# Context attentions as one block: normalisation, operands and, in the first, the combination of routed rows

## The reference, cut to what matters

```python
x = x + _L1_ffn_ref(_layernorm(x), ...)     # each row to one expert of 8, times its probability
x = x + _L2_xattn_ref(_layernorm(x), ctx, ctx, mask, ...)
...
x = x + _L3_xattn_ref(_layernorm(x), ctx, ctx, mask, attn_bias, ...)
x = x + _L3_ffn_ref(_layernorm(x), ...)

# both context attentions: q from x, k and v from the context (77 rows for each of B = 2 sequences)
q = split_heads(queries @ Wq + bq); k = split_heads(keys @ Wk + bk); v = split_heads(values @ Wv + bv)
scores = q @ k.T / sqrt(HD)      # 16 heads of HD = 16
ctx = softmax(masked scores) @ v;  return ctx @ Wo + bo
```

## Time and profile before

| | us |
|---|---|
| executions, median of 3 | 3460.03 |
| lowest, highest | 3453.24, 3462.03 |
| the profiled execution, its own time | 3466.94 |
| its span, first to last instruction | 3465.3 |

### The profile page before, as it was taken

One profiled execution on the slowest core, in us unless ns is written; L12 is line 12 of the kernel. 1 busy time (PEld: TensorE's weight loads), 2 busy tenths in 40 slices (PEclk: granted clock), 3 DMA queues, 4 the chain that ended last, 5 costly groups with the idle time before them and its releaser, 6 DMA issues. The chain is left out here.

```text
span 3465.3 us, 68349 instructions
## 1 busy us (share of the span) xinstructions
PE 2923.5 (84%) x26674; PEld 2032.6 (59%) x26675; DVE 2086.9 (60%) x3094; ACT 1894.2 (55%) x2864; POOL 1298.7 (37%) x941
## 2 busy tenths in 40 slices
PE   6679997735779998979998595979999999988596
PEld 3246665314436666536666595666666666657595
DVE  6968887485768774867783223756444444466222
ACT  3458885282448885548884111656555555456131
POOL 2259996020127885237873212630000000045212
PEclk9979998867889999989998798979999999989698
DMA  4511111100012220022222511011000000042612
GB/s 160 209 54 54 54 56 59 73 0 19 13 43 55 53 53 22 1 48 59 53 50 77 176 36 51 2 31 49 25 25 25 26 25 1 1 102 50 234 36 68
DMA packets 218052, 193.21 MB, mean 56 GB/s; under 512 B 126837, under 2 KB 176865, under 8 KB 216737
## 3 DMA queue, kind: packets, MB, share of 16 engines
q1 hardware_dynamic: 210247, 172.30, 17.2%
q0 software_dynamic: 5280, 14.42, 1.3%
q10 hardware_dynamic: 2233, 2.39, 0.2%
HBM read 112.72 MB, written 39.00 MB: 44 GB/s over the span
## 5 line engine op out<-in xcount | busy, mean ns | idle before, releaser
L2578 POOL TENSOR_TENSOR lta_p_lo<-lta_p,lta_p_hi 128x1024 f16<-128x1024 f32 x256 | 538.9, 2132 | 221.6 <-DVE lta_p_hi L2701 221.6
L2773 ACT ACTIVATE lta_p<-lta_banks,lt_gmax 128x512 f32<-128x512 f32 x512 | 323.7, 682 | 113.0 <-PE lta_banks L2616 108.5
L2684 DVE TENSOR_REDUCE lta_s_ps<-lta_s_ps 128x1 f32<-128x1101 f32 x240 | 314.2, 1309 | 106.8 <-PE lta_s_ps L2595 106.8
L3717 PE MATMUL m_h_ps<-m_x,m_w 128*128 128x512 f16 x1536 | 356.5, 383 | 4.1 <-issue 4.1
L3729 PE MATMUL m_y_ps<-m_w,m_hT 128*128 128x256 f16 x3072 | 355.8, 273 | 2.3 <-DVE m_hT L3887 2.3
L3887 DVE TENSOR_TENSOR m_hT<-m_h,m_hT 128x512 f16<-128x512 f32 x256 | 177.0, 692 | 281.1 <-ACT m_hT L3814 279.4
L3814 ACT ACTIVATE m_h<-m_h_ps,m_h_bias,m_h_scale 128x512 f32<-128x512 f32 x256 | 199.3, 778 | 266.0 <-PE m_h_ps L3717 257.8
L3729 PEld LDWEIGHTS m_y_ps<-m_w,m_hT 128*128 128x128 f16 x3072 | 298.9, 98 | 65.9 <-issue 8.6
L1227 POOL TENSOR_TENSOR c0a_tri_p_lo<-c0a_tri_p,c0a_tri_p_hi 128x1024 f16<-128x1024 f32 (+2 forms) x192 | 285.5, 1524 | 58.5 <-DVE c0a_tri_p_hi L1401 57.8
L3717 PEld LDWEIGHTS m_h_ps<-m_x,m_w 128*128 128x128 f16 x1536 | 151.1, 99 | 163.0 <-issue 10.6
L1476 ACT ACTIVATE c0a_tri_p<-c0a_banks,c_size 128x512 f32<-128x512 f32 (+3 forms) x384 | 208.3, 576 | 45.6 <-PE c0a_banks L1295 34.3
(11 more groups left out here) (758 smaller groups left out, 6574.7 us busy)
## 6 DMA issues: line engine op xcount, KB each, us to landing
m_w<-in_L_ffn_w_dram SPq DMA_DIRECT2D x4, 8192.0 KB, 39.0
m_raw<-in_L_ffn_W_dram SPq DMA_DIRECT2D x16, 1024.0 KB, 6.5
lta_q<-ltb_qT SPq DMA_DIRECT2D x96, 128.0 KB, 2.4
c_side<-in_fside_Bx16xSxS_dram SPq DMA_DIRECT2D x16, 616.0 KB, 4.9
c0a_tri_q<-c_near SPq DMA_DIRECT2D x96, 96.0 KB
c0a_tri_k<-c_mixed SPq DMA_DIRECT2D x93, 96.0 KB
lta_k<-ltb_kT SPq DMA_DIRECT2D x64, 137.6 KB, 2.5
lt_vh<-ltb_v SPq DMA_DIRECT2D x64, 128.0 KB
```

Source lines behind the costliest of these rows:

```text
L2578: nc.gpsimd.tensor_tensor(p_lo[:, slot, :], p32[:, p32_slot(h, j), :], p_hi[:, slot, :], ALU.subtract).then_inc(rested, 1)
L2684: nc.vector.tensor_reduce(ntop_of(h)[:, n:n + 1], scores(h, n), AX_X, ALU.max, negate=True).then_inc(top_ready, 1)
L2773: nc.scalar.activation(p32[0:rows, slot, c * 512:(c + 1) * 512], t_ps[0:rows, c, :], ACT.Exp, bias=bias, scale=p["gmax"][0:rows, 0:1]).the ...
L3717: last = nc.tensor.matmul(h_ps[:, f % RING, :], w1[:, v, a, c, f * P:(f + 1) * P], x16[:, b, c, n * CHUNK:(n + 1) * CHUNK], start=c == 0 a ...
```

## The change

The separate normalisation block of the context attentions goes; `cross_operands` becomes one block that normalises, turns and projects in four groups of four tiles (`CHUNK = 4`). In the first attention (`combine` is given) the combination of the routed rows is part of the same block as well: GpSimd issues the gathers there, VectorE combines and sums four tiles, makes their statistics, and ScalarE normalises the tiles of groups 0 to 2 (by a shift and a scale), VectorE those of group 3. The context's keys and values come first on TensorE, and each group's queries directly behind its turned tiles (`lag` 0). In the second attention the statistics stay one chain and VectorE normalises all tiles; keys and values come behind the first group of turned tiles, and a group's queries behind the next group's (`lag` 1). In both, the last group's queries stand behind the maximum of the values, which is now taken over partitions by a transpose, a VectorE maximum over 128 numbers, and a product that spreads it (the all-reduce on GpSimd goes). Queries have a ring of two banks, turned tiles one of three. Every load has its own semaphore. The products that make `kbd` move from VectorE to GpSimd; two memsets move the other way. `slot` and `weight` live outside the feed-forward's stage, so that stage is left ahead of the combination; for the last feed-forward `combine_experts` is called behind it and computes as before.

```diff
-def routed_ffn_stage(nc, env, tag, args, name, func, biased, capacity, out=None):
+def routed_ffn_stage(nc, env, tag, args, name, func, biased, capacity, slot, weight):
...
-        slot = st.sb("slot", [P, TILES], U32)
-        weight = st.sb("weight", [P, TILES])
...
-        with ExitStack() as inner:
-            combine_experts(nc, env, Stage(nc, inner, tag + "c"), inner, sorted_y, slot, weight, out)
+    return sorted_y
...
-def combine_experts(nc, env, st, ctx, sorted_y, slot, weight, out):
...
+def combine_experts(nc, env, tag, sorted_y, slot, weight, out):
+    with ExitStack() as ctx:
+        st = Stage(nc, ctx, tag)
+        yg = st.sb("yg", [P, TILES, D])
+        gathered = env.gathered.pop()
+        added, stored = st.sem("added"), st.sem("stored")
+        block = ctx.enter_context(nc.Block())
...
-            if out is None:
-                dve.wait_ge(added, t + 1)
-                nc.vector.bn_stats(env.stats[:, t, :], env.x[:, t, :]).then_inc(summed, 1)
-        dve.wait_ge(added, TILES)
-        if out is None:
-            dve.wait_ge(summed, TILES)
...
-def cross_attention_stage(nc, env, tag, args, name, mask, side, hides):
+def cross_attention_stage(nc, env, tag, args, name, mask, side, hides, combine=None):
...
+    CHUNK, TURNED, NORMED = 4, 3, 4
+    groups = T // 512
+    lag = 1 if combine is None else 0
...
-    layernorm_stage(nc, env, st.tag + "l", env.x, dst_T=xT)
+    rows = sb("rows", [P, NORMED, D])
...
-        sp.dma_start(wk[:], mat("Wk")).then_inc(kv_loaded, 16)
-        sp.dma_start(wv[:], mat("Wv")).then_inc(kv_loaded, 16)
-        sp.dma_start(bk[:], col("bk"), allow_slow_non_contiguous=True).then_inc(kv_loaded, 16)
-        sp.dma_start(bv[:], w("bv").partition_broadcast(P)).then_inc(kv_loaded, 16)
-        sp.dma_start(wq[:], mat("Wq")).then_inc(q_loaded, 16)
-        sp.dma_start(bq[:], col("bq"), allow_slow_non_contiguous=True).then_inc(q_loaded, 16)
+        sp.dma_start(wk[:], mat("Wk")).then_inc(wk_loaded, 16)
+        sp.dma_start(wv[:], mat("Wv")).then_inc(wv_loaded, 16)
+        sp.dma_start(wq[:], mat("Wq")).then_inc(wq_loaded, 16)
+        sp.dma_start(bq[:], col("bq"), allow_slow_non_contiguous=True).then_inc(bq_loaded, 16)
+        sp.dma_start(bk[:], col("bk"), allow_slow_non_contiguous=True).then_inc(bk_loaded, 16)
+        sp.dma_start(bv[:], w("bv").partition_broadcast(P)).then_inc(bv_loaded, 16)
...
-        nc.gpsimd.memset(v_top[:], 0.0).then_inc(v_set, 1)
-        nc.gpsimd.memset(v16[:, :, :, HD:HD + 1], 1.0).then_inc(v_set, 1)
...
+        if combine is not None:
+            for t in range(TILES):
+                nc.gpsimd.indirect_dma_start(yg[:, t, :], None, sorted_y, bass.IndirectOffsetOnAxis(ap=slot[:, t:t + 1], axis=0)
+                                             ).then_inc(gathered[t], 16)
...
-        pool.wait_ge(v_topped, 1)
-        nc.gpsimd.partition_all_reduce(v_max[:], v_top[:], P, RMAX).then_inc(v_reduced, 1)
+        pool.wait_ge(ind_made, 1)
+        for c in range(DC):
+            pool.wait_ge(k_ready, c + 1)
+            for b in range(B):
+                nc.gpsimd.tensor_tensor(kbd[:, c, b, :].rearrange("p (h j) -> p h j", h=half),
+                                        spread(kT[:, c:c + 1, b * NCTX:(b + 1) * NCTX], [P, half, NCTX]),
+                                        spread(ind[:, :].unsqueeze(2), [P, half, NCTX]), ALU.mult).then_inc(kbd_ready, 1)
+        pool.wait_ge(kbd_ready, DC * B)
...
+        def turn(t):
+            pe.wait_ge(normed, t + 1)
+            if t >= TURNED:
+                pe.wait_ge(x_evac, t - TURNED + 1)
+            for c in range(DC):
+                last = nc.tensor.transpose(x_ps[:, t % TURNED, c * P:(c + 1) * P], rows[:, t % NORMED, c * P:(c + 1) * P],
+                                           env.ident[:])
+            last.then_inc(x_turned, 1)
+
+        def queries(n):
+            if n == 0:
+                pe.wait_ge(wq_loaded, 16)
+            pe.wait_ge(x_evac, CHUNK * (n + 1))
+            for f in range(DC):
+                i = DC * n + f
+                if i >= 2:
+                    pe.wait_ge(q_evac, i - 1)
+                for c in range(DC):
+                    last = nc.tensor.matmul(q_ps[:, i % 2, :], wq[:, c, f * P:(f + 1) * P], xT[:, c, n * 512:(n + 1) * 512],
+                                            start=c == 0, stop=c == DC - 1)
+                last.then_inc(q_done, 1)
+
+        def context():
+            pe.wait_ge(wk_loaded, 16)
+            pe.wait_ge(ctx_evac, 1)
+            for f in range(DC):
+                for c in range(DC):
+                    last = nc.tensor.matmul(k_ps[:, f * B * NCTX:(f + 1) * B * NCTX], wk[:, c, f * P:(f + 1) * P],
+                                            ctxT[:, c, :], start=c == 0, stop=c == DC - 1)
+            last.then_inc(k_done, 1)
+            pe.wait_ge(wv_loaded, 16)
...
+        if lag == 0:
+            context()
+        for g in range(groups):
+            for t in tiles_of(g):
+                turn(t)
+            if g == 0 and lag == 1:
+                context()
+            if g >= lag and g < groups - 1:
+                queries(g - lag)
+        if lag == 1:
+            queries(groups - 2)
+        pe.wait_ge(v_topped, 1)
+        nc.tensor.transpose(c_ps[0:1, 0:P], v_top[:], env.ident[:]).then_inc(top_turned, 1)
+        pe.wait_ge(peaked, 1)
+        nc.tensor.matmul(c_ps[:, P:P + 1], env.ones[0:1, :], peak[0:1, 0:1], start=True, stop=True).then_inc(peak_spread, 1)
+        queries(groups - 1)
...
+        def spread_std(g, part):
+            act.wait_ge(var_ready, g + 1)
+            nc.scalar.activation(rstd[:, part], var[:, part], ACT.Sqrt).then_inc(std_ready, 1)
+
+        def normalise(t):
+            if t >= NORMED:
+                act.wait_ge(x_turned, t - NORMED + 1)
+            nc.scalar.activation(rows[:, t % NORMED, :], env.x[:, t, :], ACT.Identity, bias=shift[:, t:t + 1],
+                                 scale=rstd[:, t:t + 1]).then_inc(normed, 1)
+
+        def keep_rows(t):
+            act.wait_ge(x_turned, t + 1)
...
+        if combine is None:
+            spread_std(0, slice(0, TILES))
+        for g in range(groups):
+            if combine is not None:
+                spread_std(g, slice(g * CHUNK, (g + 1) * CHUNK))
+                if g < groups - 1:
+                    act.wait_ge(rstd_ready, 2 * (g + 1))
+                    for t in tiles_of(g):
+                        normalise(t)
+            for t in tiles_of(g):
+                keep_rows(t)
+            if g:
+                keep_queries(g - 1)
+        keep_queries(groups - 1)
...
+        def group_stats(g, part):
+            merge_stats(nc, step, mean[:, part], var[:, part], env.stats[:, part, :], D)
+            nc.vector.tensor_scalar(var[:, part], var[:, part], LN_EPS, None, ALU.add).then_inc(var_ready, 1)
+            dve.wait_ge(std_ready, g + 1)
+            nc.vector.reciprocal(rstd[:, part], rstd[:, part]).then_inc(rstd_ready, 1)
+            dve.wait_ge(rstd_ready, SHIFTED * g + 1)
+
+        def complete(t):
+            dve.wait_ge(gathered[t], 16)
+            nc.vector.scalar_tensor_tensor(env.x[:, t, :], yg[:, t, :], weight[:, t:t + 1], env.x[:, t, :], ALU.mult,
+                                           ALU.add).then_inc(added, 1)
+            if t % CHUNK:
+                sum_row(t - 1)
+
+        def sum_row(t):
+            dve.wait_ge(added, t + 1)
+            nc.vector.bn_stats(env.stats[:, t, :], env.x[:, t, :]).then_inc(summed, 1)
+
+        def scale_bias():
+            dve.wait_ge(bq_loaded, 16)
+            nc.vector.tensor_scalar(bqs[:], bq[:], HD ** -0.5, None, ALU.mult).then_inc(bqs_ready, 1)
+
+        def normalise(t):
+            if t >= NORMED:
+                dve.wait_ge(x_turned, t - NORMED + 1)
+            nc.vector.tensor_scalar(rows[:, t % NORMED, :], env.x[:, t, :], mean[:, t:t + 1], rstd[:, t:t + 1],
+                                    ALU.subtract, ALU.mult).then_inc(normed, 1)
...
+        def halve_values():
+            link = chain(dve, v_linked)
+            dve.wait_ge(top_turned, 1)
+            nc.vector.tensor_reduce(peak[:], c_ps[0:1, 0:P], AX_X, ALU.max).then_inc(peaked, 1)
+            dve.wait_ge(peak_spread, 1)
+            link(nc.vector.tensor_scalar(v_max[:], c_ps[:, P:P + 1], TINY, None, ALU.max))
...
+        nc.vector.memset(v_top[:], 0.0).then_inc(v_set, 1)
+        nc.vector.memset(v16[:, :, :, HD:HD + 1], 1.0).then_inc(v_set, 1)
+        if combine is None:
+            SHIFTED = 1
+            group_stats(0, slice(0, TILES))
+            for t in range(TILES):
+                normalise(t)
+                if t == 8:
+                    scale_bias()
+                if t == 12:
+                    keep_values()
+            keep_keys()
+            halve_values()
+            hide()
         else:
...
+            SHIFTED = 2
+            for g in range(groups):
+                part = slice(g * CHUNK, (g + 1) * CHUNK)
```

(24 more changed lines are left out.)

158 lines of the change are left out of this document (74 added, 84 removed).

## The result

| | us |
|---|---|
| before, median of 4 (lowest, highest) | 3460.23 (3453.24, 3462.03) |
| changed, median of 4 (lowest, highest) | 3435.89 (3432.49, 3441.12) |
| ratio, 95% interval | 0.9935, 0.9914 to 0.9955 |
| the changed kernel's profiled execution, its span | 3441.12, 3439.5 |

24.3 us faster by the medians; 26 were forecast, and the time lies in the forecast's range. The profiled execution is the slowest of the four.

A forecast was written before the change was run, and what follows sets the result against it. Bounds: GpSimd's gathers in the combination, then barriers and load waits, TensorE at the operands' end. Gains of 18.7 (Part A) and 7.7 (Part B), 26.4, taken as 26, off median 3460 gave 3434 us; range 3425 to 3446.

The forecast's parts named there:

- Part A: Routed rows' combination, normalisation and operands of the first context attention: 59.6 us, to gain 18.7, bounds 14 to 20.5.
- Step 1: Before the first gather: clear moved ahead of the combination, +0.4, and GpSimd's constant, +0.5 us.
- Step 2: First four tiles: fourth gather issued 3.8 later, combined 2.8 after issue; loads delaying first gathers 0.5 (0 to 2).
- Steps 2 to 4: VectorE's groups: 0.99 a tile, statistics chain 2.03, shift 0.21, so 6.2 a group; VectorE takes over from gathers' 5.03.
- ScalarE is free when a root is asked for: First attention: ScalarE normalises 12 tiles, about 0.4 each, and no root has to wait for it.
- Steps 5 to 7: First attention's tail: last tiles normalised 1.46, keys, values, maximum's hop 0.9, last queries 3.47, copy, clear; GpSimd products hidden.
- The clock: First attention: 1.0 us taken off for query group 3 of 4 meeting a slow TensorE clock (0 to 3.5).
- R1: Rival: every first-attention query group runs at 1.2 GHz, 6.9 us a group; time 3438.5; chance 0.10.
- R3: Rival: gathers starve, their issues held by VectorE's two-input SBUF reads; gain gone at 3.4 a gather; chance 0.05.
- Part B: Normalisation and operands of the last context attention, TensorE the bound: 37.5 us, to gain 7.7, bounds 5 to 9.5.
- R2: Rival: last attention wins nothing, turns between query groups each stalling TensorE two us; time 3441; chance 0.06.
- R4: Rival: no overlap, no group normalised or projected until all sixteen tiles are combined; time 3452; chance 0.02.

The follow-up runs named there:

- again: The changed kernel run once more, unedited, beside the follow-up kernels: 3436.65 us, ratio 0.9925 to the kernel before.
- plain_rows: Changed kernel with the 16 indirect gathers replaced by plain transfers on SP, rows' permutation left out (measurement only): 3434.06 us, ratio 0.9913.
- a_end: Changed kernel with query groups 0 to 2 of the first context attention placed behind all turned tiles and row copies: 3445.32 us, ratio 0.9957.
- loads_late: Changed kernel with SP's loads from wq on held until the fourth gather has landed, first attention: 3438.3 us, ratio 0.9931.
- preload: Changed kernel with the first attention's seven loads issued in the routed feed-forward behind the expert weights, into own buffers: 3460.5 us, ratio 0.9991.

## Why the prediction was right, point by point

The time came out 2 us from the forecast, but in A errors of opposite sign met, and the closeness is in part luck: the medians differ by 0.6 to 3.5 more than the two stretches account for. Times after the first gather:

| | predicted | changed | again |
|---|---|---|---|
| chain of group 0 starts | 8.0 | 10.8 | 11.2 |
| group 1 | 14.4 | 15.9 | 16.2 |
| group 2 | 20.6 | 24.9 | 23.6 |
| group 3 | 26.8 | 29.8 | 28.8 |
| last tiles' normalisation starts | 28.9 | 34.4 | 31.7 |
| last queries start | 33.4 | 39.7 | 36.9 |
| table load | 38.5 | 45.0 | 42.3 |

**Part A.**
- Step 1 (+0.9 before the first gather): from store to gather 6.28 in place of 5.54, +0.7. Right.
- Step 2 (first group 8.0 after the first gather): my 8.0 has a slip of 0.4, since its terms give 3.8+2.8+1.0 = 7.6. Measured are 7.8 in the three runs that keep most or all loads away from the first gathers, so the gathers' pace was read rightly, but the loads cost 2.8 and 3.2 over the 8.0, above my upper bound of 2. Yet moving them gained nothing, since TensorE and ScalarE reached the second query group no sooner.
- Steps 2 to 4 (0.99 a tile, 6.2 a group, VectorE the bound): **the failed step**. Without waits between them combination and sum overlap their starts: four tiles take 3.01 (2152.23 to the chain at 2155.24), 0.75 each, and the group 4.95. VectorE keeps up with the gathers' 5.03 rather than taking over. The variances were ready 6.3, 7.7 and 5.0 apart, not 6.2 each, because of the gaps. I had read 0.99 from rows in which each instruction waits for the one before it.
- What sets the pace from the second query group on is TensorE with ScalarE, 6.0 a group with warm queries (2158.54 back to 2152.54 in the repetition): 3.5 of queries, 1.34 of turns, 1.14 for a bank. I had put the bank wait down only in B. Nearly equal to my 6.2, it hid the error; the group had another master.
- "ScalarE is free when a root is asked for" was wrong for the last one: VectorE waits 1.33 for it with warm queries ahead (again, `plain_rows`), 3.03 with slow ones, and 0.27 with none (`a_end`). It didn't matter, since TensorE was still busy.
- Steps 5 to 7: from the last normalisation to the last queries 5.2 in place of 4.55 (hop 1.3 in place of 0.9, of it 0.28 a bank), from there to the table load 5.35 in place of 5.1. The four products on GpSimd took 1.22 each, 4.76 in all (1.29 and 5.2 forecast), and were hidden.
- The clock (1.0, up to 3.5): the first query group ran at the lower level in every run with queries between the turns, the second too in the changed kernel (5.37) and four others, not in its repetition (3.67). That is 1.7 of the 2.7 between the two profiles; the other 1.0 was there when the second group began. So R1 came in part, within the bounds. (The rise that I put 3.3 us behind TensorE's start came 3.5 behind it by the earlier trace rows: 0.80 in the us from 2155 is 2155.4, and the start is 2151.95.) R3 did not: gathers were issued 1.257 apart, as before, and at most 1.285 in the other kernels.
- VectorE has idle gaps of 2 to 4 us in all, 15 to 25 after the first gather, in every kernel with gathers in the block (in `loads_late` the most of them at 12 to 16, where late gathers may be the cause), even with no queries beside (`a_end`); ScalarE has some too (above, in `preload`). No step had them. They vanish with the gathers; they didn't appear where the combination stood alone, either. What makes them is **open**: transfers, issues and the long unbroken row of VectorE's instructions fall together there, and I have not separated them, nor tested whether the engines waited for instructions.

A gained 13.9 and 16.6 against 18.7 and bounds of 14 to 20.5: the first just misses the lower bound. From first gather to table load it took 45.0 and 42.3, where I had written 40 to 43.

**Part B.** Gain 6.9 to 7.6 over four kernels against 7.7 (bounds 5 to 9.5), each step as written: first turned tile 0.5 after the normalisation starts at 3019.73, context 4.54 (4.6), group 4.98 (4.87), hop 0.95 (0.9). R2 is excluded: the stall is 0.48 a group, not two us. R4 is excluded by TensorE's queries at 2142.08, before the last gather was issued.

**Sum.** 26 taken; 20.8 and 23.7 in the two stretches, 24.3 by the medians, 15.6 to 29.8 by the interval.

## What to carry to other kernels

Take the price of an instruction that will be queued without waits from rows where it is queued so; a pitch read between waits (0.99 against 0.75) makes the wrong engine the bound. In a block that several engines share, go through each engine's list in order for what it will be behind (here the last root behind copies that wait for queries), and then ask who waits for it at that time: VectorE sat idle for 3.03 and it cost nothing, because TensorE was busy for longer. Interleaving pays where the engine pauses (8.7 us in A) and not where it is full (about 1 in B); and before a load is moved earlier, look at what its queue already holds and which barrier the issuing engine owes.

## What the runs showed of the hardware

- A load issued behind 16 MB of others on SP blocks the issuing engine for 31 us; the landing would have mattered to no one, but the blocked engine held a barrier, and the stretch from the gate's load to the first expert rows grew by 22.6 us (78.4 against 55.8), by 2.0 with the same loads ahead of the 16 MB.
- 1.05 MB of plain loads make single indirect gathers up to 2.9 us later (5.65 against 2.78 from issue to use), without changing their issue, 1.257 apart. With the loads out of the way the first group is back at 7.8 (three kernels).
- The same VectorE instruction takes 1.12 us while GpSimd multiplies and 0.48 when it doesn't. Row of the first attention and of the second, changed kernel:

```profile
2165.59 1.12 DVE L3509 TENSOR_SCALAR c_v<-c2p_v,c2p_v_size 77x512 f16<-77x512 f32 x1
```
```profile
3042.90 0.48 DVE L3509 TENSOR_SCALAR c_v<-c3p_v,c3p_v_size 77x512 f16<-77x512 f32 x1
```

  GpSimd's products ran to 2166.43 in the first and to 3039.50 in the second. The Trainium skill ("SBUF — State Buffer", SBUF: two separate sides) says that whichever starts first, a GpSimd instruction or a VectorE instruction in a 2-port mode (or one with two inputs in SBUF, against a GpSimd instruction that reads SBUF), gets the port pair that the two share for its whole length, and the other waits. By that the loss is at most one product, 1.22, and the 0.64 measured agrees. Not every instruction suffers: the maximum of the values took 0.68 beside the products (at 2162.49) and 0.682 without them. Which VectorE instruction works in such a mode no run here shows. It lay beside TensorE's queries and cost nothing here. The combinations beside the gathers' issues, feared in R3, show no such stretch: 0.47 to 0.48 each, as alone.
